# Layer-1 experts: selection padded to 128 columns, and both halves of the router weight in one product

## What is computed

```python
def _L1_ffn_ref(x, norm_w, w1, w3, w2, gate_w, a1, b1, a3, b3, a2, b2):   # F=512, E=8, R=16, K=2, SCALING=2
    t = (x * rsqrt(mean(x * x) + EPS) * norm_w).reshape(-1, 128)
    probs = softmax(t @ gate_w.T)                       # 8 experts
    topw, topi = top_k(probs, 2); topw = topw / sum(topw)
    weights = sum(one_hot(topi, 8) * topw[..., None], axis=1)
    h1 = t @ w1.T + 2 * (t @ a1[e].T) @ b1[e].T         # one for each expert e
    h3 = t @ w3.T + 2 * (t @ a3[e].T) @ b3[e].T
    act = silu(h1) * h3
    out_e = act @ w2.T + 2 * (act @ a2[e].T) @ b2[e].T
    return sum(weights[e] * out_e[e])

x = x + _L1_ffn_ref(_layernorm(x), ...)
```

## Time and profile before

| | |
|---|---|
| median of the three runs | 944.12 us |
| span of the profiled execution, first to last instruction | 943.2 us |
| its own time beyond the span | not recorded; the median stands 0.9 us above the span |
| TensorE products busy | 870.1 us (92%) |
| TensorE weight loads | 577.1 us (61%) |
| VectorE | 730.4 us (77%) |
| ScalarE | 538.8 us (57%) |
| GpSimd | 466.1 us (49%) |
| mean granted TensorE clock | 0.976 of full |
| one turn of the experts, between the selection transposes at 722.44 and 755.98 us | 33.55 us |

### The profile page before, as it was taken

The page is one execution under the profiler, slowest core; times in us unless marked ns, Lnnn a source line. Parts: engine busy times, 40 slices in busy tenths (PEclk is TensorE's granted clock), DMA queues, the critical chain, the costliest instruction groups (busy, mean ns, idle before and its releaser), DMA issues. The chain is left out here.

```text
span 943.2 us, 18314 instructions
## 1 busy us (share of the span) xinstructions
PE 870.1 (92%) x6457; PEld 577.1 (61%) x6457; DVE 730.4 (77%) x1479; ACT 538.8 (57%) x794; POOL 466.1 (49%) x620
## 2 busy tenths in 40 slices
PE   5999999998878786799999999998899999999997
PEld 4777777775666664345454544443557766766775
DVE  5888998879899995988988989897665646555542
ACT  4577788789466665377777777767423123222311
POOL 4033223224668786255666666455464355345444
PEclk9899999999999998689999999999999999999999
DMA  9200000000000007745446445200000000000000
GB/s 282 80 12 12 11 11 11 11 1 0 5 1 12 13 1 148 151 101 125 106 86 134 91 98 106 49 4 15 12 1 24 12 11 22 22 0 22 11 12 11
DMA packets 35639, 43.35 MB, mean 46 GB/s; under 512 B 4825, under 2 KB 27769, under 8 KB 35569
## 3 DMA queue, kind: packets, MB, share of 16 engines
q1 hardware_dynamic: 35569, 42.43, 18.8%
HBM read 21.21 MB, written 15.07 MB: 38 GB/s over the span
## 5 line engine op out<-in xcount | busy, mean ns | idle before, releaser
L1857 ACT ACTIVATE PT<-PS 128x1024 f32<-128x1024 f32 x160 | 162.8, 1023 | 56.2 <-PE PS L1642 55.9
L1920 POOL TENSOR_SCALAR_AFFINE_SELECT PT<-PT 128x256 f32<-128x256 f32 (+1 forms) x224 | 97.4, 451 | 108.0 <-ACT PT L1857 105.5
L2347 POOL TENSOR_TENSOR PRE_sb<-PRE_sb,VA 128x512 f32<-128x512 f32 x64 | 82.4, 1287 | 132.3 <-DVE PRE_sb L2415 132.2
L2313 ACT ACTIVATE sg_d<-PS 128x512 f32<-128x512 f32 x64 | 38.3, 598 | 159.7 <-PE PS L1381 159.7
L2415 DVE TENSOR_TENSOR PRE_sb<-sg_d,PS 128x512 f32<-128x512 f32 x64 | 43.9, 688 | 85.2 <-ACT sg_d L2313 84.7
L459 ACT ACTIVATE E<-PS,m 128x512 f32<-128x512 f32 x128 | 85.8, 688 | 37.2 <-PE PS L345 28.4
L1960 DVE TENSOR_REDUCE negm<-PS 128x2 f32<-128x1024 f32 x64 | 77.9, 1222 | 22.6 <-PE PS L1631 21.6
L1657 PE MATMUL PS<-PT,VA 128*32 128x512 f32 (+3 forms) x1024 | 89.5, 445 | 0.7 <-POOL PT L1920 0.7
L1627 PE MATMUL PS<-kS,qS 48*128 48x384 bf16 (+3 forms) x512 | 74.9, 316 | 9.2 <-ACT PT L1857 2.9
L508 POOL TENSOR_SCALAR Qs<-Qs 128x1024 f32<-128x1024 f32 x32 | 34.4, 1076 | 82.9 <-ACT Qs L440 82.4
L1963 DVE TENSOR_REDUCE negm<-PS 128x2 f32<-128x768 f32 x64 | 61.2, 956 | 10.9 <-PE PS L1631 9.5
(11 more groups left out here) (333 smaller groups left out, 2316.1 us busy)
## 6 DMA issues: line engine op xcount, KB each, us to landing
qk_rows<-parts SPq DMA_DIRECT2D x32, 192.0 KB, 2.7
qS<-qk_rows SPq DMA_DIRECT2D x32, 192.0 KB, 4.3
kS<-qk_rows SPq DMA_DIRECT2D x32, 192.0 KB, 4.7
xs_sb<-XN_sb SPq DMA_DIRECT2D x20, 256.0 KB, 2.3
qk_rows<-parts SPq DMA_DIRECT2D x32, 128.0 KB, 2.8
X_sb<-in_x_dram SPq DMA_DIRECT2D x8, 256.0 KB, 6.0
qk_rows<-parts SPq DMA_DIRECT2D x32, 64.0 KB, 2.5
out_dram<-X_sb SPq DMA_DIRECT2D x8, 256.0 KB, 2.3
```

What stands on the lines that cost most here:

```text
L1857: nc.scalar.activation(PT[:, quad % 2, u, :], PS[:, b:b + 2, :].rearrange("p b n -> p (b n)"), ACT.Exp).then_inc(exp_ready, 1)
L1920: nc.gpsimd.affine_select(out=v, in_=v, pattern=[[0, 4 if u == 4 else 2], [1, P]], compare_op=ALU.is_ge, fill=0.0, base=0, channel_multipl ...
L2347: nc.gpsimd.tensor_tensor(acts[:, s, f, :], acts[:, s, f, :], W[:, slot, s, :], ALU.mult).then_inc(weighted, 1)
```

## The change

The selection has 128 columns instead of 22; the added ones are cleared once and stay zero. With it, the transposed selection and the table `spread` have 128 rows. The router weight's two halves stand side by side in one matrix of 16 columns. Per tile one product of the high half of x gives both, in 16 columns of the result, and a second product adds the low half of x by the high weight to the upper 8. The two groups of 8 are added when they are read: VectorE does that with a reduction (`add_logits`), in place of ScalarE's copy (`keep_logits`).

```diff
-    NS = 22
-        self.spread = sb("spread", [self.NS, 4, P], BF16)
+        self.spread = sb("spread", [P, 4, P], BF16)
-        self.sel = sb("sel", [P, NT, self.NS], BF16)
-        self.selT = sb("selT", [self.NS, S], BF16)
+        self.sel = sb("sel", [P, NT, P], BF16)
+        self.selT = sb("selT", [P, S], BF16)
...
+        self.gw_both = sb("gw", [P, 2 * E1], F32R)
+        self.gw = self.gw_both[:, 0:E1], self.gw_both[:, E1:2 * E1]
...
         for t in range(NT):
-            dst, ts_ = self.g.PS[:, 0, t * E1:(t + 1) * E1], slice(t * P, (t + 1) * P)
-            self.nc.tensor.matmul(dst, self.xTl[:, slot, ts_], self.gw[0][:, :], start=True, stop=False)
-            self.nc.tensor.matmul(dst, self.xTh[:, slot, ts_], self.gw[0][:, :], start=False, stop=False)
-            ins = self.nc.tensor.matmul(dst, self.xTh[:, slot, ts_], self.gw[1][:, :], start=False, stop=True)
+            dst, ts_ = self.g.PS[:, 0, 2 * t * E1:2 * (t + 1) * E1], slice(t * P, (t + 1) * P)
+            self.nc.tensor.matmul(dst, self.xTh[:, slot, ts_], self.gw_both[:, :], start=True, stop=False)
+            ins = self.nc.tensor.matmul(dst[:, E1:2 * E1], self.xTl[:, slot, ts_], self.gw[0], start=False, stop=True)
         ins.then_inc(self.logits_ready, 1)
...
-        tgt = self.g.PS[0:self.NS, 0, :].bitcast(BF16)
+        tgt = self.g.PS[:, 0, :].bitcast(BF16)
...
-    def keep_logits(self, act, i):
-        act.wait_ge(self.logits_ready, i + 1)
-        self.nc.scalar.activation(self.lg[:, :, :], self.g.PS[:, 0, 0:NT * E1].rearrange("p (t e) -> p t e", e=E1), ACT.Copy).then_inc(self.lg_ready, 1)
+    def add_logits(self, dve, i):
+        dve.wait_ge(self.logits_ready, i + 1)
+        parts = self.g.PS[:, 0, 0:2 * NT * E1].rearrange("p (t k e) -> p t e k", k=2, e=E1)
+        self.nc.vector.tensor_reduce(self.lg[:, :, :], parts, AX.X, ALU.add).then_inc(self.lg_ready, 1)
...
             nc.scalar.activation(ex.spread[:, :, :], g.spread_f[:, :, :], ACT.Copy).then_inc(consts, 1)
+            nc.scalar.activation(ex.sel[:, :, :], ident[:, :].unsqueeze(1).broadcast_to([P, NT, P]), ACT.Copy, scale=0.0).then_inc(consts, 1)
...
-                ch.base = 2
+                ch.base = 3
+                ch.wait()
...
                     if n == 0:
                         ex.keep_x(act, i + 1, 1 - slot)
                     elif n == 1:
-                        ex.keep_logits(act, i + 1)
                         keep_u(i + 1)
                         ex.second_weight(act, i + 1)
...
                         if not last:
+                            ex.add_logits(dve, i + 1)
                             ex.rank_experts(dve, i + 1)
                             keep_u_low(i + 1)
                             ex.select(dve, i + 1)
...
-        g.spread_f = sb("spread_f", [22, 4, P])
+        g.spread_f = sb("spread_f", [P, 4, P])
...
-    sp = np.zeros((22, 4, P), np.float32)
+    sp = np.zeros((P, 4, P), np.float32)
```

More of the change, by code:

```diff
@@ L1342, in two @@
             return sb(name + "h", list(whole.shape), F32R), sb(name + "l", list(whole.shape), F32R)
-        self.w1, self.b1, self.a1, self.a3, self.gw = (two(n, whole) for n, whole in (
-            ("w1", g.w1t), ("b1", g.b1t), ("a1", g.a1t), ("a3", g.a3t), ("gw", g.gwt)))
+        self.w1, self.b1, self.a1, self.a3 = (two(n, whole) for n, whole in (
+            ("w1", g.w1t), ("b1", g.b1t), ("a1", g.a1t), ("a3", g.a3t)))
+        self.gw_both = sb("gw", [P, 2 * E1], F32R)
+        self.gw = self.gw_both[:, 0:E1], self.gw_both[:, E1:2 * E1]
         self.split = [(g.gwt, self.gw), (g.a1t, self.a1), (g.a3t, self.a3), (g.w1t, self.w1), (g.b1t, self.b1)]
@@ L1880, in period @@
                             ex.keep_x(act, 0, 0)
-                        elif (quad, u) == (1, 4):
-                            ex.keep_logits(act, 0)
                     elif last and (quad, u) == (0, 4):
@@ L2043, in keep_selection @@
                 dve.wait_ge(ex.sel_turned, 1)
-                nc.vector.tensor_copy(ex.selT[:, :], PS[0:ex.NS, 0, :].bitcast(BF16)[:, 0:S]).then_inc(ex.selT_ready, 1)
+                nc.vector.tensor_copy(ex.selT[:, :], PS[:, 0, :].bitcast(BF16)[:, 0:S]).then_inc(ex.selT_ready, 1)
             def keep_mask(k):
@@ L2087, in period @@
                         ex.keep_x_low(dve, 0, 0)
+                    elif opens(i, 1) and (quad, u) == (1, 4):
+                        ex.add_logits(dve, 0)
                     elif opens(i, 1) and (quad, u) == (2, 4):
@@ L2296, in keep_selection @@
                 act.wait_ge(ex.sel_turned, i + 1)
-                nc.scalar.activation(ex.selT[:, :], PS[0:ex.NS, 0, :].bitcast(BF16)[:, 0:S], ACT.Copy).then_inc(selT_ready, 1)
+                nc.scalar.activation(ex.selT[:, :], PS[:, 0, :].bitcast(BF16)[:, 0:S], ACT.Copy).then_inc(selT_ready, 1)
             def keep_mask(i, slot, k):
```

## The result

| | before | after |
|---|---|---|
| median of six runs | 943.99 us | 933.72 us |
| lowest and highest of these | 939.54, 945.81 | 932.59, 937.99 |
| span of the profiled execution | 943.2 | 936.2 |
| time of the profiled execution | not recorded | 937.99 |
| TensorE products busy | 870.1 (92%) | 861.3 (92%) |

The recorded ratio is 0.9911, with a 95% interval of 0.9886 to 0.9935: faster by about 1%.

What follows compares the result with a forecast made beforehand. In the last stage TensorE's instruction stream was taken to set the time. Gains of 4.1 + 1.4 + 0.75 + 0.36 = 6.6 us, off the runs' median of 944.12, gave 937.5 us, range 934.7 to 941.0.

Steps and rivals of the forecast that it cites:

- Masks, 4.1 us: Mask pairs between full-size f32r products lose their partition-change pauses: 0.29 us per pair, 14 pairs in seven turns, 4.1 us.
- Rival (b): Pauses around the masks come from the bf16 type and stay; masks and transposes gain nothing: 943.0 us, chance 0.10.
- Selection transposes, 1.4 us: The four selection transposes on TensorE take 0.28 us in place of 0.52: six turns x 0.24, 1.4 us.
- Logits, 0.75 us: TensorE does 0.45 us less per turn, but VectorE's chain lets only 0.15 be kept in five turns: 0.75 us.
- Logits in attention, 0.36 us: Once, at 617 us, VectorE waits for TensorE's logits; its maximum starts 0.36 us earlier, bounds 0 and 0.45.
- Sum: All four gains, 4.1 + 1.4 + 0.75 + 0.36 = 6.6 us, giving 937.5 us.
- Costs set at nothing: ScalarE's clearing of the selection and the longer mask-table load, 0.6 us each without cover, were expected to hide.
- rival (c): VectorE's new reduction is held by GpSimd too, so its chain ends about 0.45 us later: 940.7 us, chance 0.09.
- (d): Longer TensorE waits let the granted clock fall in each of six turns, costing 10 us: 947.7 us, chance 0.03.
- Rival (a): The logits' saving is kept whole, ranking not held by GpSimd or more slack: 2.4 us more, 935.1, chance 0.13.

Runs made afterwards that it cites:

- logits_only: The kernel before with only the new logits (8 products and VectorE's reduction, selection still 22 columns): steady turn 33.38 us against 33.55, median 943.15 us.
- masks_only: The changed kernel with the old logits (twelve products, ScalarE's copy), so the padding alone: steady turn 32.75 us, median 940.00 us.

## Where the prediction was right, and where not

- *Masks, 4.1 us.* 0.28 per pair in place of 0.29, 14 pairs: 3.9. The first turn, where only masks count, is 35.04 in place of logits_only's 35.60: 0.56 for two pairs. Rival (b), the type, falls by the full-array bf16 masks; the reading of the earlier trace rows, that the change of partition is what costs, is now shown from the other side by 64 rows.
- *Selection transposes, 1.4 us.* 0.304 in place of the expected 0.28: 0.22 a turn, 1.3 us. By the rule of the Trainium skill (TensorE: Matmul & The Clock Gate, "LDWEIGHTS"), 107 ns for each load of 128 columns, four loads would take an estimated 0.43 us. The trace disagrees: the whole group is through in 0.304, and its products start 0.06 apart (0.40 for four less 0.23 for one, over three), as they did with 22 columns.
- *Logits, 0.75 us.* The steps held: the chain bound, the first ranking step held by GpSimd (0.43 without it), 0.30 lost at h(4), nothing gained in the first turn. Mis-sized is the count. I excluded the sixth turn because a(2) followed the addition directly there; logits_only gains 0.16 in each turn from 709.20 on, so 6 x 0.16 = 1.0. What set the sixth turn apart is an idle time of 0.17 in VectorE's chain, where the other turns have 0.03. It stands in both profiles of the kernel before and in masks_only, and is gone with the new logits:

```profile
748.29 0.23 DVE L1445 TENSOR_TENSOR ohl<-oh,lg 128x64 f32<-128x64 f32 x1 [0.17 <-DVE oh L1444]
```

- *Logits in attention, 0.36 us.* logits_only needs 239.55 from first exponential to first ranking step, before 240.10, changed 239.59: about 0.5, which is no more than executions differ by (239.07 to 239.59 in the changed kernel's three). So I read it at the place itself: the maximum starts at 618.47 in place of 619.04, in an execution that was 0.14 ahead before 616 us: 0.43.
- *Sum.* 3.9 + 1.3 + 1.0 + 0.43 = 6.6, as forecast, though two terms were a little too large and two too small; the marks give 6.3 behind 637 us, and the place in attention 0.43 before.
- *Costs set at nothing.* ScalarE's clearing took 0.62 at 384.95 and its wait of 3.08 became 2.52. VectorE's reduction took 0.22, so rival (c) falls. The granted clock is 1.00 from 700 to 930 us with the longer waits of 0.74, so (d) falls in the steady turns. Rival (a) falls by the same 0.74.
- *The step that failed* is the level from which the sum starts, "the runs' median of 944.12 stands 0.9 above the span, which I carry over". I took the profiled execution of before and its distance from the median as the level for both kernels, and carried over 0.9 between span and time; in the executions whose profile has a time it is 1.7 to 1.8. Between the two profiled executions, which reach attention at the same time (397.34 and 397.27), the prediction hits (937.5 against 937.99), in part by luck: with 1.8 for the 0.9 it would have been 938.4, and the two spans differ by 7.0, not 6.6; the median of after fell into the better pattern, whose lowest run is 5.4 below the profiled one. The range of 934.7 to 941.0 counted unknown costs of the change and had nothing for that, so the median fell out of it, though the change was worth what the sum said.

## What to carry to other kernels

A short product that uses part of the array, between full-array ones, pays for the change into that part and back, here 0.28 us for a pair of masks; padding its operands with zeros to 128 rows and columns removes that, while half the array removes none of it. Before counting a saving on the engine that seems to bind, follow what the next wait hangs on: here two thirds of the logits' gain stopped at a chain of another engine, and moving one addition out of that chain brought it back. Compare kernels by stretches between marks that both traces share, when whole executions differ by more than the change.

## What the runs showed of the hardware that I had not expected

- The granted clock differs between executions of one program in the same place, behind nearly the same idle time (0.54 and 1.00 from 256.6 to 263 us, behind 2.56 and 2.22 us idle of 4). The stretch around it, from 191 to some 325 us, took 136.5 to 137.0 us in the seven profiles with such a fall, and 132.6 in the four with none.
- A late fall of the clock cost more than a shorter wait gave: with the first wait at 1.9 in place of 2.7 us, the fall to 1.2 GHz came at 687.8 in place of 683.7 and lasted to 694.6 in place of 687.1, and the turn grew by 1.8 to 2.0 us in three profiles of three. Two profiles without that edit have the late fall as well, so that the shorter wait causes it is not shown.
- A product with 64 rows is followed and preceded by the same pause as one with 22 (0.734 and 0.73 for the pair).
